# Graph network kernel: adjacency columns loaded by halves over spent low parts, and layer 3's MLP tiles reordered

## The reference

```python
# layer 1: attention over the adjacency's pattern
z = x @ W.T + bW
e = leaky(ai + aj.T)                     # ai, aj: one value for each node
att = softmax(where(adj > 0, e, -9e15) with a sink column)
out = att @ z
# layer 2: GIN
h = relu(((1 + eps) * x + adj @ x) @ W1 + b1);  out = h @ W2 + b2       # 512 hidden
# layer 3: GIN with RMS norm
h = (epsilon * x + adj @ x) @ W1 + b1                                     # 1024 hidden
out = silu(h * rsqrt(mean(h**2) + 1e-6) * w) @ W2 + b2
```

## Time and profile before

| quantity | value |
|---|---|
| median of 3 runs | 3128.87 us (3128.55 to 3129.03) |
| profiled execution, its own time | 3128.71 us |
| its span in the profile | 3126.9 us |
| granted TensorE clock, mean over the span | 0.975 of full speed |
| busy: PE, DVE, ACT, POOL | 93%, 67%, 42%, 30% |
| one graph, from a point of one to the same point of the next | about 180 us |

### The profile page before, as it was taken

The page is one execution under the profiler, slowest core; times in us unless marked ns, Lnnn a source line. Parts: engine busy times, 40 slices in busy tenths (PEclk is TensorE's granted clock), DMA queues, the critical chain, the costliest instruction groups (busy, mean ns, idle before and its releaser), DMA issues.

```text
span 3126.9 us, 39949 instructions
## 1 busy us (share of the span) xinstructions
PE 2895.4 (93%) x14794; PEld 2443.2 (78%) x14794; DVE 2087.2 (67%) x4580; ACT 1325.3 (42%) x2468; POOL 924.6 (30%) x1088
## 2 busy tenths in 40 slices
PE   4729999999999999999999999999999999999997
PEld 4617888888888888888888888888888888888886
DVE  3267667685867758586776858676676858677533
ACT  0222634436253543535254453526344362535423
POOL 1103333242233224223322323233332422332230
PEclk8959999999999999999999999999999999999998
DMA  4023040211304030130403012040402113040100
GB/s 131 6 88 115 1 128 8 77 59 34 102 1 135 1 108 28 41 95 1 135 1 115 21 51 86 5 131 1 127 9 77 59 32 104 1 135 1 41 14 14
DMA packets 203441, 180.94 MB, mean 58 GB/s; under 512 B 15568, under 2 KB 184944, under 8 KB 203248
## 3 DMA queue, kind: packets, MB, share of 16 engines
q1 hardware_dynamic: 62560, 109.94, 10.3%
q10 hardware_dynamic: 140688, 68.46, 7.7%
HBM read 161.17 MB, written 17.19 MB: 57 GB/s over the span
## 4 chain that ended last, share of the span: by engine, by line
PE 76%; DVE 10%; ACT 3%; POOL 3%; issue 2%; DMA 0%; ACTq 0%; SPq 0%; POOLq 0%; DVEq 0%
PE bank L728 21%; PE bank L712 18%; PE bank L669 9%; PE bank L671 9%; PE bank L670 9%; PE bank L637 3%; DVE mt_lo L1085 2%; PE bank L628 2%; DVE stat L1128 2%; POOL x_lo L1004 1%; PE bank L697 1%; PE bank L749 1%; PE bank L648 1%; ACT mt_hi L842 1%; DVE a_lo L1099 1%
## 5 line engine op out<-in xcount | busy, mean ns | idle before, releaser
L728 PE MATMUL bank<-W,hid 128*128 128x256 f32 x3072 | 697.2, 381 | 15.1 <-ACT hid L912 15.1
L728 PEld LDWEIGHTS bank<-W,hid 128*128 128x128 f32 x3072 | 581.0, 191 | 100.1 <-issue 18.7
L669 PE MATMUL bank<-mt_hi,x_hi 128*128 128x512 f32 x1536 | 637.5, 415 | 0.0
L671 PE MATMUL bank<-mt_hi,x_lo 128*128 128x512 f32 x1536 | 604.9, 394 | 0.0
L670 PE MATMUL bank<-mt_lo,x_hi 128*128 128x512 f32 x1536 | 602.2, 392 | 0.0
L842 ACT ACTIVATE mt_hi<-bank 128x512 fp32r<-128x512 f32 x512 | 279.4, 598 | 584.6 <-PE bank L637 548.0
L1206 DVE TENSOR_TENSOR sq_sum<-sq_sum,scratch 128x512 f32<-128x512 f32 x224 | 155.1, 693 | 374.8 <-ACT scratch L907 374.8
L999 POOL TENSOR_TENSOR rstd<-ve,neg_half 128x4 f32<-128x4 f32 x128 | 130.1, 1017 | 912.0 <-DVE ve L1136 911.9
L1085 DVE TENSOR_TENSOR mt_lo<-bank,mt_hi 128x512 fp32r<-128x512 f32 x512 | 329.6, 685 | 84.6 <-ACT mt_hi L842 83.0
L671 PEld LDWEIGHTS bank<-mt_hi,x_lo 128*128 128x128 f32 x1536 | 290.2, 189 | 64.7
L712 PE MATMUL bank<-a_hi,W_hi 128*128 128x512 f32 x768 | 340.4, 443 | 0.0
(11 more groups left out here) (139 smaller groups left out, 4612.5 us busy)
## 6 DMA issues: line engine op xcount, KB each, us to landing
adj_col<-in_adj ACTq DMA_DIRECT2D x128, 512.0 KB, 3.9
att<-in_adj SPq DMA_DIRECT2D x128, 512.0 KB, 7.5
out<-x_even SPq DMA_DIRECT2D x64, 128.0 KB, 2.4
out<-x_odd SPq DMA_DIRECT2D x64, 128.0 KB, 1.9
x_even<-in_x SPq DMA_DIRECT2D x56, 128.0 KB, 4.5
x_odd<-in_x SPq DMA_DIRECT2D x56, 128.0 KB, 4.4
G<-in_L_gnn_W SPq DMA_DIRECT2D x2, 2560.0 KB, 14.4
W_f<-in_L_gnn_W SPq DMA_DIRECT2D x1, 1024.0 KB, 9.8
```

The lines of the kernel that those rows point to most:

```text
L669: nc.tensor.matmul(dst[:], hi, mt_hi[:, k, cols], start=k == 0, stop=False)
L671: mm = nc.tensor.matmul(dst[:], lo, mt_hi[:, k, cols], start=False, stop=done and not extra)
L728: mm = nc.tensor.matmul(out_bank[t // 2][:, t % 2 * D:(t % 2 + 1) * D], src[:, t * P:(t + 1) * P], W2[:, m, :], start=(m == 0 and t % 2 == ...
```

## The change

Five things are done.

1. `adj_col` becomes a whole 1024 x 1024 matrix laid over `mt_lo`. A half column tile (k, h), 256 KB, is loaded by SP into the place of the attention's low part (k, h) as soon as `agg_step(1, k, h)` has read it (semaphore `s_att_used`). There are 16 such loads in place of 8 from ACT's queue, and they stand in SP's list among the stores and loads of x and of attention rows.
2. `turn_col` transposes a half tile (four blocks, one bank). Six of the 16 stand between the second steps, five in layer 1's second half, five in layer 2. Layer 2's order becomes steps (0..3, half 0), (0..3, half 1), (4..7, half 0), (4..7, half 1); `attention_out` of half 1 comes after step (1, 0), and `aj_rows` after step (4, 1).
3. ACT, DVE and POOL lists are rearranged to match. On DVE `agg_lo(2, 0)` goes ahead of `aj_copy`, three scores and not four stand ahead of `agg_lo(2, 1)`, and the mask of scores 4 and 5 is made between `statistics` and `normalize`.
4. In layer 3 the RMS row goes to another bank, needs only the first of the two `a_lo` tiles of half 1, and comes after `turn_att` 3; each hidden tile of half 1 goes ahead of the second step of half 0, and ACT waits for that second step ahead of writing `hid` again.
5. `a_hi` and `a_lo` signal for each of their two tiles.

```diff
-    adj_col = sb("adj_col", [P, CR, NT, P])
-    mt_hi, mt_lo = sb("mt_hi", [P, NT, NODES], F32R), sb("mt_lo", [P, NT, NODES], F32R)
+    mt_hi = sb("mt_hi", [P, NT, NODES], F32R)
+    with ExitStack() as place:
+        adj_col = sb("adj_col", [P, NT, NODES], F32, place)
+    mt_lo = sb("mt_lo", [P, NT, NODES], F32R)
...
-    sum_bank, row_bank = banks[6], banks[3]
+    sum_bank, row_bank = banks[6], banks[2]
...
+    COL_AT = {0: (6, 0), 1: (7, 0), 4: (0, 1), 5: (1, 1), 6: (2, 1)}
...
+            def load_col(b, k, h):
+                if k < NT - 1:
+                    sp.wait_ge(s_att_used, used_count(b, k, h))
+                else:
+                    sp.wait_ge(s_agg, agg_count(b, 1, h))
...
+                sp.dma_start(dst, src).then_inc(s_col_in[k][h], 16)
...
+                for k in range(NT - 1):
+                    load_col(b, k, 0)
                 if not first:
                     for t in tiles(0):
                         store(b - 1, t, 1 - buf)
+                load_col(b, NT - 1, 0)
+                if not last:
+                    load_xs(b + 1, tiles(0), 1 - buf, first)
...
                 if not first:
                     for m in range(HT3):
                         second_step(b - 1, 3, 1, m)
+                        if m >= 2:
+                            turn_col(b, m - 2, 0)
+                else:
+                    for k in range(6):
+                        turn_col(b, k, 0)
                 for k in range(NT):
                     agg_step(1, k, 1)
-                    if k % 2 == 1:
-                        turn_col(b, k // 2)
-                    if k == 3:
+                    if k in COL_AT:
+                        turn_col(b, *COL_AT[k])
+                    if k == 2:
                         attention_out(b, 0, first)
...
+                for k in range(4):
+                    step_2(k, 0)
+                    if k == 1:
+                        attention_out(b, 1, first)
+                    if k > 0:
+                        turn_col(b, k + 2, 1)
+                for k in range(4):
+                    step_2(k, 1)
+                    if k < 2:
+                        turn_col(b, k + 6, 1)
+                for k in range(4, NT):
+                    step_2(k, 0)
+                for k in range(4, NT):
+                    step_2(k, 1)
+                    if k == 4 and not last:
                         aj_rows(b + 1, False)
...
-                for k in range(6, NT):
-                    agg_step(3, k, 1)
+                if not last:
+                    turn_att(b + 1, 2)
+                agg_step(3, 6, 1)
                 rms_sum(b, 0)
-                if not last:
-                    turn_att(b + 1, 2)
+                agg_step(3, 7, 1)
+                if not last:
+                    turn_att(b + 1, 3)
                 rms_row(b, 0)
-                if not last:
-                    turn_att(b + 1, 3)
+                a_ready(b, 3, 1)
                 for m in range(HT3):
+                    hidden_tile(b, 3, 1, m)
                     second_step(b, 3, 0, m)
-                    hidden_tile(b, 3, 1, m)
```

More of the change, by code:

```diff
@@ L16 @@
 HALF = 512
-CR = 2
 HID2, HID3 = 512, 1024
@@ L595, in graph @@
                         store(b - 1, t, 1 - buf)
+                for k in range(4, 6):
+                    load_col(b, k, 1)
                 if not last:
-                    for t in tiles(1):
-                        if first:
-                            load_x(b + 1, t, 1 - buf)
-                        else:
-                            next_x(b + 1, t, 1 - buf)
+                    load_xs(b + 1, tiles(1), 1 - buf, first)
+                for k in range(6, NT):
+                    load_col(b, k, 1)
                 if not last:
@@ L731, in second_step @@
                         mm.then_inc(s_out, 1)
+                if layer == 3 and h == 0 and m < HT3 - 1:
+                    mm.then_inc(s_hid_used, 1)
             def rms_sum(b, h):
@@ L941, in graph @@
                 if not last:
-                    for t in range(1, 4):
+                    for t in range(1, 3):
                         exp(b + 1, t)
@@ L1030, in graph @@
                     rstd_of(b - 1, 3, 0)
-                diagonal(b, 0)
-                diagonal(b, 1)
+                for k in range(4):
+                    diagonal(b, k)
                 for t in range(NT):
@@ L1039, in graph @@
                 rstd_of(b, 1, 0)
-                diagonal(b, 2)
                 for t in tiles(0):
                     x_low(b, 1, t, buf)
-                diagonal(b, 3)
-                diagonal(b, 4)
+                for k in range(4, NT):
+                    diagonal(b, k)
                 rstd_of(b, 1, 1)
@@ L1230, in graph @@
                 agg_lo(b, 1, 0)
+                turn_col_lo(b, 0, 0)
+                turn_col_lo(b, 1, 0)
                 if not last:
                     statistics(b + 1, 0, 0, 1 - buf)
+                turn_col_lo(b, 2, 0)
+                turn_col_lo(b, 3, 0)
+                if not last:
                     normalize(b + 1, 0, 0, 1 - buf)
-                if not first:
-                    residual(b - 1, 3, 1, 1 - buf)
-                    statistics(b - 1, 3, 1, 1 - buf)
-                turn_lo(b, 0, True)
+                turn_col_lo(b, 4, 0)
+                turn_col_lo(b, 5, 0)
                 if not last:
@@ L1292, in graph @@
                     if not last and m == 4:
-                        turn_lo(b + 1, 1, False)
+                        turn_lo(b + 1, 1)
+                if not last:
+                    turn_lo(b + 1, 2)
                 mean_square(b, 0)
                 agg_lo(b, 3, 1)
+                scale_hidden(b, 0, 0)
                 if not last:
-                    turn_lo(b + 1, 2, False)
-                for m in range(3):
+                    turn_lo(b + 1, 3)
+                for m in range(1, 3):
                     scale_hidden(b, 0, m)
-                if not last:
-                    turn_lo(b + 1, 3, False)
                 for m in range(HT3):
```

221 lines of the change are left out of this document (118 added, 103 removed).

## The result

| | before | after |
|---|---|---|
| time, median (range), us | 3128.71 (3127.54 to 3129.03) | 3188.86 (3188.17 to 3190.22) |
| span of the profiled execution, us | 3126.9 | 3186.6 |
| PE busy, us | 2895.4 | 2934.5 |
| mean granted clock of TensorE | 0.975 | 0.968 |

The change makes the kernel slower: ratio 1.0195, 95% interval 1.0179 to 1.0211, +60.2 us. The forecast was slower, 3168, with a range up to 3187; the time lies 2 us above the range.

A forecast was written before the change was run, and what follows sets the result against it. PE, busy 93% of the span, was taken as the bound. From 3128.7 us, -57.5 (a) + 11.5 (b) - 15.3 (c) + 58 (d) + 22.5 (e) + 12 (f) + 8 (g) = +39 gave 3168 us, range 3090 to 3187.

The forecast's parts named there:

- (a): Adjacency column transposes (L637): PE's waits for POOL's diagonal go, as half columns load earlier; 57.5 us removed.
- (b): Column transposes: 16 half turns for 8 whole ones cost PE 0.7 us more a graph, 11.5 us added.
- (c): Layer 3's RMS row and the hidden tile behind it: PE idles less, 15.3 us removed.
- (d): `aj_rows` and step (6, 0) in layer 2: DVE's chain to `aj` lags PE by 3.9 us a graph, 58 us added.
- (e): Start of layer 3: DVE's scores come late, PE waits 1.5 us a graph, 22.5 us added.
- (f): PE's clock behind the `aj` wait: half-speed stretches in four graphs of five, +12 us net, bounds 0 and 24.
- (g): First graph: no second steps cover six half turns, and graph 1's features load later; 8 us added.
- second rival: DVE's sums escape POOL or `aj` is late by at most 1 us, no clock lost: 3095 to 3120 us, chance 0.17.
- fourth rival: Small margins break at half turn (7, 1)'s bank and x part 0 ahead of layer 2: 3195 us, chance 0.07.
- The third: Rival: `aj` waits as forecast, but the clock holds and scores keep their slack; 3130 us, no change, chance 0.09.

The follow-up runs named there:

- e5: Kernel before with only the layer 3 part of the change (row on another bank, hidden tiles ahead of second steps, single `a_hi`/`a_lo` signals): 3113.78 us.
- e1: Kernel after with POOL's layer 1 bias additions held until DVE has made the next graph's `aj`: 3098.11 us, ratio 0.9907 to the kernel before.
- e10: Kernel after with `aj_rows` two steps later in PE's list, after step (6, 1): 3102.47 us, ratio 0.9923 to the kernel before.
- e4: Kernel after with four scores, not three, ahead of `agg_lo(2, 1)` on DVE: 3166.49 us, ratio 1.0127 to the kernel before.
- e12: Kernel after with the edits of e1, e4 and e6, `x_low` 6 and 7 ahead of `rstd_of`, `aj_rows` one step later, score 5 ahead of residual (2, 1): 3054.08 us.
- e3: Kernel after with the half turn of column (3, 1) alone moved ahead of layer 2: 3166.96 us, ratio 1.0133 to the kernel before.
- e6: Kernel after with graph 1's first feature loads issued ahead of the half columns: 3183.65 us, ratio 1.0181 to the kernel before.
- e2: Kernel after with 14 unused filler products on PE directly ahead of `aj_rows`: 3146.08 us, ratio 1.0063 to the kernel before.
- e7: Kernel after with all five later half turns one place earlier in PE's list: 3112.06 us, ratio 0.9954 to the kernel before.
- e11: Kernel after with 7 unused filler products on PE ahead of `aj_rows`: 3164.57 us, ratio 1.0116 to the kernel before.

## Why the prediction was right in sign and 21 us short

A middle graph can be summed from the traces: idle time by releaser, half of PE's busy time at half clock, and the rest as PE's own work at full speed. Of the 4.16 us, (a) is -3.63, (b) +0.2, (c) -0.8, (d) +4.3, (e) +1.9, (f) +1.8, and waits at half turns that the table didn't have are +0.4. In its own terms the prediction had -3.6, +0.7, -1.0, +3.9, +1.5 and +0.8. The largest error is (f)'s.

**(a)** Right: no wait for POOL's diagonal is left, and no load of a half column shows up among PE's waits (they land in 3.0 us, the median of 256; the trace before had one load of 256 KB after all, 2.7 us).

**(b)** Too high. In a middle graph PE's own work at full speed grew by 1.06 us, and 0.9 of that are the hidden parts of (e)'s waits; what is left for the half turns is 0.2 or less, the lower bound, and not 0.7: -8 us.

**(c)** Right. e5 measures 13.5 for 15.3: +2. What stays is 0.63 + 0.19 at the row and the tile behind it, where 0.55 + 0.2 stood.

**(d)** Right in mechanism and size. The table gave PE 19.7 us of own work from s and it had 19.7; it gave `aj` at s + 23.65, and `aj_rows` started at s + 24.08. The two waits are 3.75 + 0.58 = 4.3 for 3.9, 0.4 above. That is partly luck: the normalize of graph b+1 took 3.04 and not 1.75, and the rest of the chain was 0.9 shorter than the table had it. +7 us. e1 and e10 show the wait from both sides: take away the company or give PE other work, and it goes.

**(e)** Near in size, 0.7 at `turn_att` 0 and 1.2 from there to the first hidden tile (1.98 against 0.79), 1.9 for 1.5: +6 us. Of its reasons one held, that DVE has more scores behind PE's results (2.7 us later to the last exponential, as it said), though it named only the fourth score, which is worth half by e4; the other half came back with score 5 in e12. The other, that DVE starts the scores later because `aj_rows` does, had no effect: e1 brings `aj` 3.4 us sooner, and it takes the same 20.01 us to `turn_att` 0 as the kernel after (1441.99 to 1461.99 there), with 0.93 at the hidden tile. The second rival halved (e) by that reason; where its case was made, in e1, (e) stayed whole.

**(f)** The step that failed. The mechanism is right, half clock behind the wait, and its size is not: the term had +12 us net with an upper bound of 24, and the traces have +25. Gross it had 1.25 a graph, worked out from the earlier trace rows: 3.30 us of half speed in four graphs of five. In its place all 15 graphs have such a stretch, 9 of them with 6.8 us, and 36 us are lost, 2.4 a graph. The row was one behind a wait of 1.90, and I let only the frequency grow with the length of the wait, and drew the bound of 24 from the same row. A wait of 3.2, as I had it, would not have saved the term: in e3 it costs 2.1 a graph. The 7 us that I took off for the kernel before were nearly right: its trace has six stretches of 3.4 us behind waits at L637, 10 us lost. So 35.7 - 10.2 = 25.5 us stand where +12 stood: +13.

**(g)** The waits at half turns of the first graph, 10.1 against 1.4 before, make 8.7 for 8: +1. e6 takes back 6.6 of them with the loads alone.

A wait that the table didn't have, 0.37 a graph at a half turn for its bank (L682), adds 5 us. The fourth rival named the mechanism, a half turn that comes before its bank is free, but for (7, 1); in the trace it is (4, 0), between the second steps. (That rival's own sum, 3168 + 30, is 3198 and not 3195.) In sum -8 (b), +2 (c), +7 (d), +6 (e), +13 (f), +1 (g) and +5: +26, where 21 were missed. Against it stand 3.2 us less ahead of the first `aj_rows` and some 3 us less of half clock in the first graph and behind the last one, in stretches that differ from run to run. (f) is more than half of the error: had it been the 12 us that the term gave it, and all the rest as it came, the time would have been some 3176, inside the range. The range shares the fault: its upper end was the forecast's own and had no room for several terms that err to the same side, while the earlier trace rows made the clock look bounded. It was missed by 2 us only, so any of (d), (e) or (f) set right would have brought the time inside; the size of (f) is what was wrong by more than its own bounds.

Of the rivals, the second's mechanism (sums that escape POOL) didn't happen by itself, but e1 brought it about and landed at 3098, in its 3095 to 3120. The third had the waits without a loss of clock, and the scores at 5 us. e2 makes the first half of that, with (e) whole: 3146, and with the scores at 5 and not 28 it would be 3123 by the same sum, for the rival's 3130.

The sums take 0.82 to 0.84 beside POOL and 0.42 without it in e1. The Trainium skill (SBUF — State Buffer, Who interferes with whom) has DVE and GpSimd share a port pair under an exclusive lock, and the sums agree with it. By the same section `tensor_scalar`, although it reads one SBUF tensor, can take the shared pair too. The prediction overlooked that for the normalize, and the trace agrees: four tiles take 3.04 beside POOL in the kernel after and 1.39 at the same place in e12, with POOL idle.

## What to carry to other kernels

When a change takes waits away from the bounding engine, follow the next engine's list to the first result that the bounding one reads, and look what runs beside each item on that list; here one semaphore on an idle engine's list was worth 91 us, and five edits of order another 44 (e1 to e12). Price an idle gap of the matmul engine at more than its length (here from waits of 1.9 us on; one of 1.2 us cost its length alone), and take the extra from a gap as long as the expected one; where the trace has only shorter ones, the upper bound belongs well above them. Put other work into the gap before shortening the chain that ends it: moving `aj_rows` by two steps took one line and gave nearly as much as freeing the sums.

## What the runs showed of the hardware

How the granted clock goes with the length of one wait of PE, in the 15 graphs with a successor: behind 0.3 to 0.6 us (e1, e2) and 1.22 us (e7) it stayed at 1.00 in all; behind 2.1 us (e11) it fell in 6, with nothing different from the other 9 in the program; behind 3.16 us (e3) in 14, in 6 of them for 6.8 us; behind 3.75 us (after) in all 15, for 6.8 us in 9 and 3.4 in 6. Where it didn't last 6.8 us it lasted 3.4. In the kernel before, where the waits of 1.8 to 2.0 us at L637 have a shorter one some 4 us behind them, it fell behind 6 of 16. In the kernel after it fell while PE idled, 0.6 to 2.0 us ahead of the first product, in all 9 of the long kind, and at or up to 1.2 us behind that product in 5 of the 6 short ones.

A DVE normalize of four tiles, with one input in SBUF and scalars, is slowed by POOL's work beside it (`x_low`, then the additions) like the sums with two inputs: 3.04 us against 1.39, and 0.84 against 0.42. With `x_low` alone beside it, in e1, it takes 2.19.
